# Tail values of both batches in one product, spread by DMA: a cross-attention and mixture-of-experts kernel on one core

## What is computed

```python
x = x + xattn(layernorm(x), ctx, ctx, mask, Wq, bq, Wk, bk, Wv, bv, Wo, bo)   # x: 2 x 1024 x 256, ctx: 2 x 154 x 256
x = x + ffn(layernorm(x), ...)     # soft mixture: 16 experts x 64 slots, 256 -> 512 -> 256, gated gelu
# in xattn, 16 heads of 64:
q = (x_q @ Wq + bq); k = (x_k @ Wk + bk); v = (x_v @ Wv + bv)
s0 = jnp.where(mask, -1e30, q @ k.T / 8); p = softmax(s0)
s1 = p @ v;  return s1 @ Wo + bo
```

## Time and profile before

| | |
|---|---|
| three runs | 568.34, 565.46, 567.77 us; median 567.77 |
| profiled execution | 567.2 us, its span 565.4 us |
| granted TensorE clock, mean over the span | 0.996 |
| busy us (share of the span) | PE 537.4 (95%), PEld 502.5 (89%), DVE 453.9 (80%), ACT 395.7 (70%), POOL 312.7 (55%) |
| DMA | 51.78 MB, mean 92 GB/s |
| chain that ended last, by engine | PE 62%, DVE 14%, POOL 10%, ACT 7%, issue 5%, DMA 2% |

### The profile page before, as it was taken

One profiled execution on the slowest core, in us unless ns is written; L12 is line 12 of the kernel. 1 busy time (PEld: TensorE's weight loads), 2 busy tenths in 40 slices (PEclk: granted clock), 3 DMA queues, 4 the chain that ended last, 5 costly groups with the idle time before them and its releaser, 6 DMA issues.

```text
span 565.4 us, 11969 instructions
## 1 busy us (share of the span) xinstructions
PE 537.4 (95%) x3901; PEld 502.5 (89%) x3901; DVE 453.9 (80%) x1348; ACT 395.7 (70%) x1073; POOL 312.7 (55%) x332
## 2 busy tenths in 40 slices
PE   5889999999999999999989999899989999999997
PEld 3778999999999989999978888899968788789997
DVE  6897878888797979989685998597668999995553
ACT  4976969689695959869573454688968677646662
POOL 7662554455445354544454776977398999930000
PEclk9999999999999999999999999899999999999999
DMA  8402000000030000000001433150277888516552
GB/s 266 169 1 75 2 2 2 1 2 1 2 94 2 2 2 0 3 0 2 2 2 43 181 152 148 75 192 1 73 224 265 287 281 277 196 39 187 162 175 73
DMA packets 29868, 51.78 MB, mean 92 GB/s; under 512 B 2037, under 2 KB 16465, under 8 KB 29681
## 3 DMA queue, kind: packets, MB, share of 16 engines
q1 hardware_dynamic: 29809, 51.04, 26.9%
HBM read 40.54 MB, written 10.49 MB: 90 GB/s over the span
## 4 chain that ended last, share of the span: by engine, by line
PE 62%; DVE 14%; POOL 10%; ACT 7%; issue 5%; DMA 2%; SPq 1%; POOLq 0%; ACTq 0%; DVEq 0%
PE ps L1450 8%; PE ps L1312 8%; PE ps L1482 7%; PE ps L1515 6%; PE ps L1400 6%; DVE w_gu_low L986 5%; PE ps L1433 5%; PE ps L1381 5%; PE ps L1412 4%; PE ps L1435 3%; PE ps L1574 2%; POOL prob L680 2%; ACT expo L832 2%; DVE eo_high L1260 2%; POOL w_gu_low L743 1%
## 5 line engine op out<-in xcount | busy, mean ns | idle before, releaser
L680 POOL TENSOR_TENSOR prob<-expo,prec 128x512 f32<-128x512 f32 x64 | 66.9, 1045 | 99.2 <-DVE prec L1103 98.0
L832 ACT ACTIVATE expo<-expo,nmin 128x154 f32<-128x154 f32 x256 | 106.2, 423 | 3.7 <-DVE nmin L1092 3.2
L1092 DVE CUSTOM_DVE_ANT_0 expo<-ps,maskb 128x154 f32<-128x154 f32 x256 | 69.1, 311 | 12.6 <-PE ps L1400 12.1
L1400 PE MATMUL ps<-kbd,qT_high 128*128 128x308 f32 x256 | 61.0, 322 | 0.2 <-ACT qT_high L758 0.2
L1112 DVE TENSOR_TENSOR pT_low<-ps,pT_high 128x512 fp32r<-128x512 f32 (+1 forms) x96 | 57.1, 595 | 4.1 <-ACT pT_high L846 3.5
L846 ACT CAST pT_high<-ps 128x512 fp32r<-128x512 f32 (+1 forms) x96 | 49.2, 514 | 15.2 <-PE ps L1412 11.5
L758 ACT ACTIVATE oT_high<-ps,bqv_c 128x256 fp32r<-128x256 f32 x64 | 29.9, 467 | 37.0 <-PE ps L1435 37.0
L743 POOL TENSOR_TENSOR w_gu_low<-w_raw,w_gu_high 128x1024 fp32r<-128x1024 f32 x17 | 44.7, 2632 | 11.8 <-ACT w_gu_high L790 11.7
L832 ACT ACTIVATION_READ_ACCUMULATOR expo<-expo,nmin 128x1 f32 x256 | 50.1, 196 | 0.0
L743 POOL TENSOR_TENSOR wkq_low<-w_raw,wkq_high 128x1024 fp32r<-128x1024 f32 x15 | 43.8, 2924 | 1.0 <-ACT wkq_high L790 1.0
L1400 PEld LDWEIGHTS ps<-kbd,qT_high 128*128 128x128 f32 x256 | 40.0, 190 | 0.9 <-issue 0.5
(11 more groups left out here) (237 smaller groups left out, 1772.6 us busy)
## 6 DMA issues: line engine op xcount, KB each, us to landing
logits_dram<-lsb SPq DMA_DIRECT2D x16, 512.0 KB, 2.6
w_raw<-in_L_ffn_Wg_dram SPq DMA_DIRECT2D x16, 512.0 KB, 4.4
w_raw<-in_L_ffn_Wu_dram SPq DMA_DIRECT2D x16, 512.0 KB, 4.4
w_raw<-in_L_ffn_Wd_dram SPq DMA_DIRECT2D x16, 512.0 KB, 4.5
lraw<-logits_dram SPq DMA_DIRECT2D x13, 512.0 KB, 3.8
out_dram<-gate SPq DMA_DIRECT2D x16, 128.0 KB, 2.3
wvo_raw<-in_L_xattn_Wv_dram SPq DMA_DIRECT2D x2, 512.0 KB, 6.5
x<-in_x_dram SPq DMA_DIRECT2D x1, 1024.0 KB, 11.1
```

Source lines behind the costliest of these rows:

```text
L680: pool.tensor_tensor(prob[:, n % 2, :, heads, :], expo[:, n % 2, pp, :, :, 0:P], prec[:, n % 2, pp].unsqueeze(3).to_broadcast([P, 2, 2, P] ...
L832: ins = act.activation(row, row, ACT.Exp, scale=-1.0, bias=nmin[:, n % 2, pp, j, h:h + 1], accum_out=psums[:, n % 2, pp, j, h:h + 1])
L1092: ins = dve.tensor_tensor_reduce(out=expo[:, n % 2, pp, j, h, :], in0=ps[:, s % NS, h * SK:(h + 1) * SK], in1=maskb[:, (2 * (n // QUADS) + ...
L1400: ins = pe.matmul(dst, qT[s][:, n % 2, pp, j * P:(j + 1) * P], kbd[:, b, m, p, :], start=(r == 0), stop=(r == 2))
```

## The change

The tail of the values is now one product VT c for both batches (52 rows: 26 of batch 0, 26 of batch 1), two products in all instead of four. Its left side is cT_tails, the tail columns of both batches copied once by POOL (event cTt). ACT and DVE write its halves into `tails` (52 partitions), without a mask. Eight DMAs, one for each batch and row block a, then copy from `tails` to vt the 64 columns of head a of each quad, both halves at once; vt is cleared beforehand, its batch 0 by DVE and its batch 1 by ACT, at the program's start. The first PV waits for these eight (d_tails) instead of v_low. SP issues them behind its first loads, when the last VT is drained, and ahead of the second batch of x, gain, shift and Wo. A second path would write keys to a buffer and place them by DMA, for the pairs that DIRECT leaves out; DIRECT names all eight, so every key is written directly, as before. LOW_DVE, PROLOGUE, LOADS, EARLY and the three LATER tables have new entries: among others the zeros of pairs 2 and 3 wait for the first xn, the first piece of Wq has its low half on DVE and the first of Wo on POOL, the two warm matmuls behind cT stand at the start and three instead of two stand ahead of the first Q, and K 6 comes later.

```diff
+NK = 2
-LOW_DVE = ((WK, 0), (WK, 1), (WK, 2), (WQ, 2), (WO, 0))
+LOW_DVE = ((WK, 0), (WK, 1), (WK, 2), (WQ, 0))
+DIRECT = (0, 1, 2, 3, 4, 5, 6, 7)
 PROLOGUE = [
-    ("cT", 0), ("LN", 0), ("zeros", 0), ("cT", 1), ("warm", 2), ("split", WK, 0), ("split", WQ, 0), ("bias",),
-    ("K", 0), ("XN", 0), ("K", 1), ("xT", 0, 0), ("xT", 0, 1), ("warm", 2), ("split", WK, 1), ("Q", 0, 0),
-    ("zeros", 1), ("mask",), ("split", WK, 2), ("K", 2), ("zeros", 3), ("split", WV, 0),
+    ("zeros", 0), ("warm", 2), ("cT", 0), ("cT", 1), ("LN", 0), ("split", WK, 0), ("split", WQ, 0), ("XN", 0),
+    ("bias",), ("K", 0), ("K", 1), ("xT", 0, 0), ("xT", 0, 1), ("split", WK, 1), ("mask",), ("warm", 3),
+    ("Q", 0, 0), ("K", 3), ("zeros", 1), ("split", WK, 2), ("zeros", 3), ("split", WV, 0),
 ]
 EARLY = {
...
+    ("R", 0, 1): [("K", 4), ("split", WQ, 2), ("V", 0, 0), ("K", 7), ("split", WV, 1)],
+    ("R", 1, 1): [("V", 1, 1), ("V", 0, 1)],
+    ("S", 0, 0, 1): [("Q", 0, 1), ("zeros", 2), ("K", 5)],
+    ("Q", 2, 0): [("XB", 0)],
+    ("S", 0, 0, 0): [("K", 2), ("split", WQ, 1)],
+    ("T", 0, 0): [("K", 6)],
+    ("LN", 1): [("VT", 0)],
+    ("XN", 1): [("VT", 1)],
     ("S", 4, 0, 0): [("split", WO, 1)],
+    ("S", 3, 1, 0): [("split", WO, 0)],
+    ("T", 0, 2): [("V", 1, 0)],
+    ("Q", 1, 0): [("cTt",)],
 }
...
-    vt = halves(att, "vt", [T4, B, QUADS, 4 * DH])
+    vt = sb(att, "vt", [T4, B, 2, QUADS, 4 * DH], F32R)
...
+    cT_tails = halves(pro, "cT_tails", [P, KD, B, TAIL])
+    tails = sb(pro, "tails", [B * TAIL, 2, DM], F32R)
...
         sp.dma_start(x1[:, 2:TB], x_t[:, 0, 2:TB]).then_inc(d_x_rest, 16)
+        for ev in [ev for ev in first if ev in placed_no or ev == LAST_VT]:
+            wait_used(sp, ev)
+            if ev == LAST_VT:
+                sp.wait_ge(vt_zeros, 2)
+                for b in range(B):
+                    for a in range(4):
+                        sp.dma_start(vt[a * TAIL:(a + 1) * TAIL, b, :, :, a * DH:(a + 1) * DH]
+                                     .rearrange("p s q d -> p (s q) d").bitcast(F32),
+                                     tails[b * TAIL:(b + 1) * TAIL].rearrange("p s (q a d) -> p (s q) a d", a=4, d=DH)
+                                     [:, :, a, :].bitcast(F32)).then_inc(d_tails, 16)
...
+                if ev[1]:
+                    pool.wait_ge(xn_ready, 1)
...
+            elif ev[0] == "cTt":
+                wait_used(pool, LAST_CT)
+                for half in range(2):
+                    ins = pool.tensor_copy(cT_tails[half][:], cT[half][:, :, :, P:SK])
+                ins.then_inc(tails_ready, 1)
...
+        act.wait_ge(const_pool, 1)
+        act.activation(vt[:, 1].rearrange("p s q (a d) -> p (s q a) d", d=P),
+                       ident[0:T4].unsqueeze(1).to_broadcast([T4, 2 * QUADS * 2, P]), ACT.Identity, scale=0.0)\
+            .then_inc(vt_zeros, 1)
...
+            elif ev[0] == "VT":
+                high_half(ev, tails[:, 0, ev[1] * F:(ev[1] + 1) * F], acc(no)[0:B * TAIL, :])
...
+        dve.memset(vt[:, 0].rearrange("p s q n -> p (s q n)").bitcast(F32), 0.0).then_inc(vt_zeros, 1)
...
+            elif ev[0] == "VT":
+                cols = slice(ev[1] * F, (ev[1] + 1) * F)
+                low_half(ev, tails[:, 1, cols], acc(no)[0:B * TAIL, :], tails[:, 0, cols])
...
                 if n == 0:
-                    pe.wait_ge(v_low, 2 * B)
+                    pe.wait_ge(d_tails, 16 * 4 * B)
                     pe.wait_ge(vm_zeros, 2)
                     wait_used(pe, LAST_V)
```

More of the change, by code:

```diff
@@ L70 @@
     "R1": 1, "SA": -0.5, "S10": -1, "T1": 5, "Q0": 1, "SB": -2, ("zeros", 0): -3, "PV1": 3, "Q1": 1, "XN": -3,
-    "xT1": -0.5, "T0": 2, "Y1": -2, ("XB", 0): -1, ("split", WV, 0): 2, ("VH", 0, 0): -3, ("V", 1, 1, 1): -1,
-    ("xT", 0, 0): 1,
+    "xT1": -0.5, "T0": 2, "Y1": -2, ("XB", 0): -1, ("split", WV, 0): 3, ("xT", 0, 0): 1, ("bias",): 1,
+    ("K", 1): -1, ("K", 2): -1, ("V", 0, 0): -3, ("warm", 2): -1, ("split", WK, 2): -2, ("cT", 0): -2,
 }
@@ L212, in program @@
     order_dve, order_act, order_pool = (later(before_ffn, by) for by in (LATER_DVE, LATER_ACT, LATER_POOL))
-    first = [ev for ev in prologue + attention if ev[0] in ("K", "V")]
+    first = [ev for ev in prologue + attention if ev[0] in ("K", "V", "VT")]
     assert sorted(first) == sorted([("K", p) for p in range(PAIRS)] + [
-        ("V", b, c, t) for b in range(B) for c in range(2) for t in range(2)])
-    LAST_K, LAST_V = [[ev for ev in first if ev[0] == kind][-1] for kind in ("K", "V")]
+        ("V", b, c) for b in range(B) for c in range(2)] + [("VT", c) for c in range(2)])
+    LAST_K, LAST_V, LAST_VT = [[ev for ev in first if ev[0] in kinds][-1] for kinds in (("K",), ("V", "VT"), ("VT",))]
+    placed = [ev for ev in first if ev[0] == "K" and ev[1] not in DIRECT]
+    placed_no = {ev: i for i, ev in enumerate(placed)}
     FIRST_K = [ev for ev in first if ev[0] == "K"][0]
@@ L268, in program @@
     in_order(order_pool, r_no)
-    for kind, order in (("VH", order_act), ("VL", order_dve)):
-        in_order(order, {(kind, b, c): no for (_, b, c, _), no in tail_no.items()})
     for by, kinds in ((LATER_SLOTS_ACT, "x2T L E H sT C"), (LATER_SLOTS_DVE, "x2T N2 L A H D sT MX MB C"),
@@ L535, in values_over @@
         wait_done(eng, LAST_V)
-        eng.wait_ge(v_low, 2 * B)
+        eng.wait_ge(d_tails, 16 * 4 * B)
+        for ev in placed:
+            eng.wait_ge(d_keys[ev], 32)
     block = top.enter_context(nc.Block())
@@ L804, in step @@
                 wait_done(act, ev)
+                if ev in placed_no:
+                    if placed_no[ev] >= NK:
+                        act.wait_ge(d_keys[placed[placed_no[ev] - NK]], 32)
+                    act.activation(keys[:, placed_no[ev] % NK, :, 0], acc(no)[:, 0:B * SK].rearrange("p (b s) -> p b s", b=B),
+                                   ACT.Identity, bias=bk_c[:, p:p + 1]).then_inc(acc_high, 1)
+                    return
                 for at, cols, src in key_blocks(p, acc(no)):
@@ L1025, in step @@
                 dve.wait_ge(acc_high, high_no[ev] + 1)
+                if ev in placed_no:
+                    half = keys[:, placed_no[ev] % NK]
+                    dve.scalar_tensor_tensor(out=half[:, :, 1], in0=acc(no)[:, 0:B * SK].rearrange("p (b s) -> p b s", b=B),
+                                             scalar=bk_c[:, p:p + 1], in1=half[:, :, 0], op0=ALU.add, op1=ALU.subtract)\
+                        .then_inc(acc_free, 1)
+                    return
                 for at, cols, src in key_blocks(p, acc(no)):
@@ L1389, in step @@
                 if n < QUADS and j == 0:
-                    wait_used(pe, ("K", p))
+                    if p in DIRECT:
+                        wait_used(pe, ("K", p))
+                    else:
+                        pe.wait_ge(d_keys["K", p], 32)
                     pe.wait_ge(zeros_ready[n], 1)
```

112 lines of the change are left out of this document (38 added, 74 removed), and 6 rows, old and new, of the table EARLY.

## The result

Timed side by side in 14 runs each, the changed kernel takes 570.72 us (568.67 to 572.15) against 567.05 (565.46 to 568.83) for the kernel before: ratio 1.0053, 95% interval 1.0042 to 1.0063 (the two medians alone stand 3.67 us, or 0.65%, apart; the last section names a part of that which may not be the change's). The forecast was 564.4, with a range up to 567.3.

The account below looks back on a forecast made before the run. TensorE, busy all the time from 50 us, was taken as the bound; an earlier first PV moves everything. PV(0,0) from 47.39 to 44.5 saves 2.9, taken as 2.8: 567.2 - 2.8 = 564.4 us, range 562.9 to 567.3.

Parts of the forecast that it names:

- last V ends: PE's value products: 7.66 us of work from 34.8, plus 0.2 bank wait, ends at 42.7; before, 45.04.
- PV(0,0) by its values: First PV product, counting only the drain of the last V and issue: can start at 44.5, before 47.39.
- the path through the start: Prologue up to value piece 1: +0.2 us on ACT, high half at 32.1, low half on POOL at 34.5, unchanged.
- The twelve matmuls gone: On PE, two tail products instead of four, twelve fewer 512-column matmuls at the same length: 2.8 us less work.
- The copied keys never run: Key copies: DIRECT names all eight pairs, so that part is no change at all.
- by 52: Wo's load behind the copies on SP: issued about 44, landing at 52 at the latest, first needed by ACT at 57.
- 7 x 0.48 = 3.4: SP's issuing of the eight tail copies from 38.1, 0.48 us each, so the last is issued at 41.5.
- the new wait: PV(0,0)'s wait for eight tail copies: issued 38.1 to 41.5, landing 2.2 later at 43.7.
- 0.8 ahead of the values: At PV(0,0): the last copy lands at 43.7, 0.8 us before the values allow the start at 44.5.
- The rival in which the copies end last: Ahead of PV(0,0): short-run copies hold the queue 0.9 us each, last lands 46.6; middle case 566.0 us, chance 0.17.
- a rival for the first 15 us: Program start: Q(0,0) and K 3 come later or PE's clock rises later; 1.3 saved, 565.9 us, chance 0.15.
- The rival on the other side: At PV(0,0): copies served one after another, 1.7 us each, start at 52.0, 4.6 later; 571.8 us, chance 0.07.

Follow-up runs that it names:

- half the copies: Changed kernel with only the first batch's four copies, the second batch's tail values left zero (computes something else): 566.38 us, ratio 0.9972 to the kernel before.
- merge alone: Changed kernel's merged tail product and eight copies, under the order tables of the kernel before: 568.06 us, ratio 0.9987 to the kernel before.
- twelve products: Changed kernel plus twelve 512-column identity matmuls ahead of the first PV's wait for the copies: 568.08 us, ratio 0.9997 to the kernel before.
- two queues: Changed kernel with the second batch's four copies issued by POOL and the first batch's by SP: 577.2 us, ratio 1.0158 to the kernel before.
- the merge with nine products: Merged tail product and eight copies under the old orders, plus nine identity matmuls ahead of the first PV's wait: 564.86 us, ratio 0.9948 to before.
- the sixteen copies: Changed kernel with sixteen half-size copies, VT(0)'s issued once it is drained, first PV waiting for those alone: 572.3 us, ratio 1.008 to the kernel before.
- K 6 back: Changed kernel with K 6 moved back ahead of value weight piece 1, nothing else: 569.75 us, ratio 1.0018 to the kernel before.
- the probe of the rows: Kernel before plus eight unused SBUF copies of 16 to 128 rows, issued singly by SP; time not read, issues 0.62 to 0.89 us.
- the probe of the shapes: Kernel before plus 17 unused SP transfers of differing rows, runs and source; time not read, median issues 0.617 to 0.913 us.
- products ahead of VT(1): Changed kernel plus twelve 512-column identity matmuls ahead of VT(1)'s wait for its bank: 570.33 us, ratio 1.0039 to the kernel before.

## Why the prediction was wrong

Step by step, forecast against after:

| | forecast | after | difference |
|---|---|---|---|
| Q(0,0) on ACT; K 3 on ACT | 15.6; 16.9 | 15.62; 16.84 | 0 |
| VT(1) starts | 34.8 | 35.09 | 0.3 |
| last V ends | 42.7 | 44.46 | 1.8 |
| PV(0,0) by its values | 44.5 | 46.1 (half the copies) | 1.6 |
| copies: start, one issue | 38.1, 0.48 | 39.26, 0.89 | 1.2, 0.41 |
| PV(0,0) | 44.5 | 48.06 | 3.6 |
| PV(0,0) to the next Q | 2.68, as before | 4.21 | 1.5 |

- **Right:** the path through the start, to 0.3 us. The twelve matmuls gone at the same length. The copied keys never run, Wo is issued at 47.97 and lands 9.9 later, at 57.9 and not by 52, but ACT first reads it at 61.22, and nobody waits for it. The rest of the attention is unchanged.
- **The step that failed** is "7 x 0.48 = 3.4" in the part on the new wait. The term was mis-sized: it was read off one load of the program's start, and it measured 0.89, 7 x 0.89 = 6.2 instead of 3.4. Before's own trace has a load of the same shape, another piece of Wq, at 0.82; the sum did not use it. That turned "0.8 ahead of the values" into 2.0 behind them (48.06, and 46.10 with half the copies). The rival in which the copies end last had the 0.9 right, and its 46.6 for the landing came out near 48, since the copies also started 1.2 late. Its reason (short runs) was wrong: one run of 2 KB a row costs 0.76 where eight of 256 bytes cost 0.83.
- **The step that was missing:** idle time on PE was priced as itself. The sum lets VT(1) wait for its bank until 34.8 and then counts it at 1.40; behind 2.46 us of idle time it took 2.59, and the S behind it was slow too. That is 1.5 us in the last V, and 1.5 more behind PV(0,0). The clock was only a rival for the first 15 us, where the path came out right to 0.3 us. The experiments with products in the wait show both prices. They also show that such a stretch comes in some executions and not in others, so its place in the forecast would have been a case with a chance.
- **The rival on the other side** (copies served one after another, 1.7 each) did not happen; slower came from 0.89 us of issue and the clock, which no case had together.
- **The sum closes:** 564.4 + 3.6 + 1.5 = 569.5 for a profile at 570.89. The other 1.4 us stand in the experts' stage, which is 86.58 long in after and 85.17 in before: see the last section. The forecast was made against a profile that did not have them.

## What to carry to other kernels

A cut that makes the bounding engine wait for something new must be priced with the queue that makes it: count the DMAs, times what an issue of that very shape costs, and give the issues to two queues in gaps that the timeline shows, ahead of any large load. In the two probes copies of 32, 48, 64 or 128 rows were 0.2 us cheaper to issue than those of 24, 26, 52 or 104. And an idle time of 2.2 to 2.6 us in this stream of matmuls cost, in many executions, 1.3 to 1.6 us more than itself, because what followed ran at the 1.2 GHz level: either shorten it or fill it.

## What the runs showed of the hardware

- **The clock falls behind short idle times, in some executions.** Idle times of 2.46 (after), 2.21 (merge alone) and 2.59 us were followed by 3 to 4 us at the 1.2 GHz level; 2.47 in two profiles of the same order (twelve products, two queues) by none. A third place is in both kernels: the 2.16 us ahead of the colmax transposes near 356 us, followed by the lower level in before and after and by none in four other profiles. There it costs 1.55 (colmax to the last nb transposes near 365: 9.14 in before, 7.57 in the merge with nine products). In the profile of the sixteen copies the level fell at 21.8 us, with no more than 1.62 us of idle time and then 0.29 ahead. Each such stretch is 0.003 of the mean clock and some 1.3 to 1.6 us: K 6 back gives 566.7 at 1.000, about 568.3 at 0.997 and about 569.9 at 0.994. What decides whether it comes is not known. Nine to twelve products on an identity in the wait kept it away from the wait in every profile that had them.
- **The experts' stage has two lengths, and before's program has shown both.** From the last slot transposes to the last hid transposes PE takes 85.17 us in before and 85.12 in the probe of the rows; it takes 86.5 to 86.6 in the probe of the shapes and in all profiles with the merge but one (87.23, with products ahead of VT(1)). The mean of POOL's w_gu_low (groups view) is 3025 ns in after and 2632 in before. In the two probes, which both run before's program there, it is (shapes first, then rows)

```profile
L764 POOL TENSOR_TENSOR w_gu_low<-w_raw,w_gu_high 128x1024 fp32r<-128x1024 f32 x17 | 51.3, 3021 | 12.9 <-ACT w_gu_high L811 12.5
```
```profile
L765 POOL TENSOR_TENSOR w_gu_low<-w_raw,w_gu_high 128x1024 fp32r<-128x1024 f32 x17 | 44.6, 2629 | 11.8 <-ACT w_gu_high L812 11.7
```

the first in a span of 566.6 us, the second of 565.4. That is 1.2 us between spans with the same mean clock, 0.997. What decides it was not tried. It bears on the result: nine of the 14 executions of before took 566.7 to 567.3, while beside the experiments before's medians were 568.2 to 568.6. If those nine had the short stage, up to 1.4 of the 3.67 us between the medians is not the change's; no trace of them tells.
